# Reordering the opening of a modulated convolution kernel on all its engines

## The reference, cut to what matters

```python
s = style @ mw.T + mb
weight = SCALE * w * s[:, None, :, None]
demod = rsqrt(sum(weight * weight, axis=(2, 3)) + EPS)
weight = weight * demod[:, :, None, None]
# four layers: same, upsample + blur, same, blur + downsample; then x = x + out
```

## Time and profile before

| what | value |
|---|---|
| median of 3 runs (lowest, highest) | 1335.65 us (1335.02, 1335.79) |
| the profiled execution | 1336.1 us |
| its span in the trace | 1334.3 us |
| TensorE (PE) busy | 1301.2 us, 98% |
| VectorE (DVE) busy | 1150.0 us, 86% |
| ScalarE (ACT) busy | 842.1 us, 63% |
| GpSimd (POOL) busy | 347.3 us, 26% |
| DMA over the span | 152 GB/s |

### The profile page before, as it was taken

One profiled execution on the slowest core, in us unless ns is written; L12 is line 12 of the kernel. 1 busy time (PEld: TensorE's weight loads), 2 busy tenths in 40 slices (PEclk: granted clock), 3 DMA queues, 4 the chain that ended last, 5 costly groups with the idle time before them and its releaser, 6 DMA issues.

```text
span 1334.3 us, 20141 instructions
## 1 busy us (share of the span) xinstructions
PE 1301.2 (98%) x6565; PEld 1077.7 (81%) x6565; DVE 1150.0 (86%) x1855; ACT 842.1 (63%) x1528; POOL 347.3 (26%) x632
## 2 busy tenths in 40 slices
PE   7799999999999999999999999999999999999998
PEld 5588878888888788888888778888888878888887
DVE  6798879998988899989889789989888788898885
ACT  5656466656564666666655566566566667877774
POOL 3214221133122221124131221121522233323221
PEclk7899999999999999999999999999999999999999
DMA  9235655546554465454556445565554257655643
GB/s 312 77 100 163 166 146 125 159 149 186 170 149 113 135 186 170 141 172 121 162 172 171 140 112 158 164 178 162 164 146 124 93 121 190 186 170 146 177 121 99
DMA packets 95368, 203.38 MB, mean 152 GB/s; under 512 B 10720, under 2 KB 12256, under 8 KB 95264
## 3 DMA queue, kind: packets, MB, share of 16 engines
q1 hardware_dynamic: 94896, 201.81, 52.7%
q10 hardware_dynamic: 368, 0.28, 0.1%
HBM read 72.39 MB, written 67.24 MB: 105 GB/s over the span
## 4 chain that ended last, share of the span: by engine, by line
PE 75%; DVE 15%; ACT 4%; issue 3%; POOL 2%; DMA 1%; SPq 0%; ACTq 0%; DVEq 0%; POOLq 0%
PE ps L463 74%; ACT kp L750 2%; DVE gl L1067 2%; DVE gf L1031 2%; DVE zl L980 2%; DVE xl L974 2%; DVE X L989 1%; DVE vf L1010 1%; DVE gf L1037 1%; ACT xh L709 1%; DVE vl L1017 1%; DVE vh L1019 1%; POOL w3q L1279 1%; DVE v L1015 0%; DVE gf L1043 0%
## 5 line engine op out<-in xcount | busy, mean ns | idle before, releaser
L463 PE MATMUL ps<-zh,gh 128*128 128x512 f32 (+1 forms) x1028 | 411.1, 400 | 16.2 <-DVE zl L980 12.2
L463 PE MATMUL ps<-zl,gh 128*128 128x512 f32 (+1 forms) x1028 | 407.5, 396 | 0.0
L721 ACT ACTIVATE zh<-ps,t_bx 128x512 fp32r<-128x512 f32 x256 | 175.7, 686 | 271.4 <-PE ps L463 267.9
L463 PE MATMUL ps<-zh,gl 128*128 128x512 f32 (+1 forms) x1028 | 283.0, 396 | 0.0
L750 ACT ACTIVATE kp<-ps,t_T1s 64x256 f32<-64x256 f32 x512 | 213.5, 465 | 102.8 <-PE ps L463 99.5
L463 PEld LDWEIGHTS ps<-zh,gh 128*128 128x128 f32 x1028 | 195.0, 190 | 70.0 <-DVE zl L980 20.7
L989 DVE SCALAR_TENSOR_TENSOR X<-ps,t_D,X 128x512 f32<-128x512 f32 x255 | 190.0, 745 | 61.9 <-PE ps L463 35.4
L974 DVE SCALAR_TENSOR_TENSOR xl<-X,t_S,xh 128x513 fp32r<-128x513 f32 x256 | 202.1, 809 | 35.0 <-ACT xh L709 32.8
L980 DVE SCALAR_TENSOR_TENSOR zl<-ps,t_bx,zh 128x512 fp32r<-128x512 f32 x256 | 190.7, 745 | 48.1 <-ACT zh L721 45.2
L463 PEld LDWEIGHTS ps<-zl,gh 128*128 128x128 f32 x1028 | 195.4, 190 | 44.6
L463 PEld LDWEIGHTS ps<-zh,gl 128*128 128x128 f32 x1028 | 194.7, 189 | 45.4
(11 more groups left out here) (204 smaller groups left out, 1541.3 us busy)
## 6 DMA issues: line engine op xcount, KB each, us to landing
out_x<-X SPq DMA_DIRECT2D x255, 256.5 KB, 4.9
X<-out_x SPq DMA_DIRECT2D x96, 513.0 KB, 7.0
gh<-gh SPq DMA_DIRECT2D x127, 240.0 KB, 3.0
gl<-gl SPq DMA_DIRECT2D x127, 240.0 KB, 3.6
X<-x_in SPq DMA_DIRECT2D x32, 513.0 KB, 7.6
pk<-taps_in SPq DMA_DIRECT2D x3, 512.0 KB, 12.0
pk<-pack_in SPq DMA_DIRECT2D x3, 352.0 KB, 11.2
pk<-sets_in SPq DMA_DIRECT2D x4, 256.0 KB, 8.4
```

The costliest lines, as they stand in the source:

```text
L463: return pe.matmul(out_ap, a, b, start=first, stop=last, skip_group_check=True)
L721: act.activation(zh[n % 2][:, ZPAD:ZPAD + M], ps[:, ZP + n % 2, :], IDENT, bias=tab["bx"][:, k, b:b + 1]).then_inc(s["zhi"], 1)
```

## The change

The opening is written anew on every engine; the loops from iteration 2 on stay as they are, but for the place of `k_products(1)` and of the loads.

- TensorE makes `k_products(0)` in front of `conv0(0)` and `conv0(1)`, and `k_products(1)` behind `convg(0)` in place of behind `convg(1)`. `v_products(0)` may begin when the first half of `w3h` is there. Three groups of products whose result is not used (6, 6 and 20 of 256 columns on `w2h`) stand behind `v_products(0)`, `conv0(1)` and `v_products(1)`.
- ScalarE splits the second layer's weights first of all; `kev(0)` is in the usual order of two halves; the copies that give `gl` to the lower half (`glo_cross`) and of the outer taps (`taps_first`) move to it from VectorE.
- VectorE filters quad 0 in one go over both slots, and no longer in two; it takes `w0l` from GpSimd; `xnew(0)` comes before `xlo(3)`, and `vfull(1)`, `vlo(1)` before `zlo(1)`.
- GpSimd makes quad 1's `w3q` in front of `w1l`.
- SyncE issues `spread(0)` in iteration 1, in front of the store of sample 0, the loads of samples 16 to 23 behind it, and the weights of blocks 1, 2 and 3 (with the samples' ends) in iterations 4, 8 and 12.

```diff
@@ before build
+BLOCK_LOADS = {4: 1, 8: 2, 12: 3}
@@ SyncE
-            for n in range(2 * GS, NR * GS, 2):
-                load(n)
-            for k in range(1, NBLK):
-                sp.dma_start(pk[:, k, 0:PACK], pack[k]).then_inc(s_pack[k], 16)
-                sp.dma_start(pk[:, k, PACK:WALL], taps[k]).then_inc(s_taps[k], 16)
...
             for n in range(NN + 4):
-                if n == 2:
+                if n == 1:
                     spread(0)
+                    for m in range(2 * GS, NR * GS, 2):
+                        load(m)
+                if n in BLOCK_LOADS:
+                    k = BLOCK_LOADS[n]
+                    sp.dma_start(pk[:, k, 0:PACK], pack[k]).then_inc(s_pack[k], 16)
+                    sp.dma_start(pk[:, k, PACK:WALL], taps[k]).then_inc(s_taps[k], 16)
...
@@ TensorE, v_products(0): high parts start on the first half of w3h
+                if q == 0:
+                    pe.wait_ge(s["w2hi"], 1)
+                    pe.wait_ge(s["w3h0"], 1)
...
@@ TensorE, the order of the opening
             v_products(0)
-            conv0(0)
+            idle_products(6, filled)
             pe.wait_ge(s["z0"], 1)
             k_products(0)
+            conv0(0)
             conv0(1)
+            idle_products(6, filled)
             v_products(1)
+            idle_products(20, filled)
             for n in range(NN):
...
                 if n == 0:
                     convg(n)
+                    k_products(1)
...
-                if n in G_LATE:
-                    k_products(g_at(n))
@@ ScalarE, from the first weights on
+            act.wait_ge(s["w1t"], 16)
+            act.activation(w1d[:, 0, 0:K], w1T[:, 0], ACT.Copy).then_inc(s["w1d0"], 1)
+            act.activation(w1h[0:C, 0, 0:K], w1T[0:C, 0], ACT.Copy)
+            act.activation(w1h[C:128, 0, 1:K + 1], w1T[C:128, 0], ACT.Copy).then_inc(s["w1hi"], 1)
...
             w0hi(0)
-            w1hi(0)
-            xhi(0)
-            act.wait_ge(s["z0"], 1)
-            root(PARTS[1], 2)
-            vhi(0)
-            xhi(1)
-            w3hi(1)
-            zhi(0)
...
-            for j in (0, 2, 1, 3):
-                evict(0, j, 0)
-                ins = evict(0, j, 1)
...
-            ghi_first(0)
-            xhi(2)
-            zhi(1)
-            ghi_first(1)
-            ghi_rest()
-            vhi(1)
-            xhi(3)
-            root(PARTS[2], 3)
-            zhi(2)
-            xhi(4)
-            kev(1, 0)
-            kev(1, 1)
+            first_var(PARTS[2])
+            root(PARTS[1], 2)
+            w3hi(1)
+            vhi(0)
+            xhi(0)
+            xhi(1)
+            kev(0, 0)
+            root(PARTS[2], 3)
+            kev(0, 1)
+            zhi(0)
+            taps_first()
+            zhi(1)
+            xhi(2)
+            xhi(3)
+            ghi_first(0)
+            vhi(1, 0)
+            glo_cross(0)
+            vhi(1, 1)
+            ghi_first(1)
+            ghi_rest()
+            glo_cross(1)
+            kev(1, 0)
+            zhi(2)
+            kev(1, 1)
+            xhi(4)
             w3hi(2)
...
@@ VectorE, behind E1
             recip(PARTS[1], 2)
             vfull(0)
-            xlo(0)
-            vlo(0)
-            newton(PARTS[1], 2)
...
-            dve.wait_ge(s["kev0"], 1)
-            fir_first(slice(0, 1), "fir0")
-            xlo(2)
-            glo_first(0)
-            dve.wait_ge(s["kev"], 1)
-            fir_first(slice(1, 2), "fir")
...
+            newton(PARTS[1], 2)
+            vlo_first()
+            dve.scalar_tensor_tensor(T0["T1s"], dall[:, 0, :], 1.0 / BLUR_SUM, dall[:, 1, :], ALU.mult, ALU.mult) \
+                .then_inc(s["t1s"], 1)
+            dve.wait_ge(s["var0"], 2)
+            recip(PARTS[2], 3)
+            dve.wait_ge(s["w0hi"], 1)
+            dve.tensor_tensor(w0l[:, 0], w0f[:, 0], w0h[:, 0].bitcast(F32), ALU.subtract).then_inc(s["w0l"], 1)
+            xlo(0)
...
             xlo(1)
+            newton(PARTS[2], 3)
+            dve.wait_ge(s["kev"], 1)
+            fir_even(whole, both, first=True)
+            fir_odd(whole, both).then_inc(s["fir"], 1)
+            zlo(0)
+            vfull(1)
+            glo_first(0)
+            xlo(2)
+            vlo(1)
+            zlo(1)
+            glo_first(1)
+            xnew(0)
+            glo_rest()
             xlo(3)
-            xnew(0)
             zlo(2)
             xlo(4)
             for n in range(2, NN):
@@ GpSimd
-            sig(pool.tensor_tensor(w0l[:, 0], w0f[:, 0], w0h[:, 0].bitcast(F32), ALU.subtract), "w0l")
...
+            pool.wait_ge(s["e1"], 1)
             w3s(1)
+            w1low()
+            pool.wait_ge(s["t1s"], 1)
             w3lo(1)
@@ new functions of ScalarE
+            def taps_first():
+                act.wait_ge(s["fir0"], 1)
+                act.activation(gf[:, 0:NT:NT - 1], kp[:, 1:8:6], ACT.Copy).then_inc(s["gfe0"], 1)
+            def glo_cross(i):
+                act.wait_ge(s[("gl0a", "gl1a")[i]], 1)
+                act.activation(gl[C:128, 0, i, 1:NT + 1, :], gl[0:C, 0, i, 0:NT, :].bitcast(F32), ACT.Copy) \
+                    .then_inc(s[("gl0", "gl1")[i]], 1)
```

More of the change, by code:

```diff
@@ L521, in v_products @@
                 left, right = slice(0, 2), slice(2, 4)
-                pe.wait_ge(s["w2l"], k + 1)
-                if q >= 1:
-                    pe.wait_ge(s["kev"], q)
[L525 to L530, removed]
+                if q == 0:
+                    pe.wait_ge(s["w2hi"], 1)
+                    pe.wait_ge(s["w3h0"], 1)
+                    add(a[:, 0], wh[:, left, :], w3h[:, 0], first=True)
+                    add(a[:, 1], wh[:, right, :], w3h[:, 0])
+                    pe.wait_ge(s["w2l"], 1)
+                    add(a[:, 0], wl[:, left, :], w3h[:, 0])
+                    add(a[:, 1], wl[:, right, :], w3h[:, 0])
+                    pe.wait_ge(s["w3l0"], 1)
+                else:
+                    pe.wait_ge(s["w2l"], k + 1)
+                    pe.wait_ge(s["kev"], q)
+                    pe.wait_ge(s["w3h"], q + 1)
+                    add(a[:, 0], wh[:, left, :], w3h[:, 0], first=True)
+                    add(a[:, 0], wl[:, left, :], w3h[:, 0])
+                    add(a[:, 1], wh[:, right, :], w3h[:, 0])
+                    add(a[:, 1], wl[:, right, :], w3h[:, 0])
+                    pe.wait_ge(s["w3l"], q + 1)
                 add(a[:, 0], wh[:, left, :], w3l[:, :, :])
@@ L544, in k_products @@
                 pairs = ((k01, early, 0), (k23, late, 0), (k23, early, 1), (k45, late, 1))
-                pe.wait_ge(s["w1l"], k + 1)
+                if q == 0:
+                    pe.wait_ge(s["w1hi"], 1)
+                    pe.wait_ge(s["w1l0"], 1)
+                else:
+                    pe.wait_ge(s["w1l"], k + 1)
                 pe.wait_ge(s["vh"], q + 1)
@@ L553, in k_products @@
                 pe.wait_ge(s["vl"], q + 1)
+                if q == 0:
+                    pe.wait_ge(s["w1l"], 1)
                 add(k45, d[:, early, :], vh[:, 2, :, :])
@@ L735, in w3hi, with first_var, vhi @@
                 act.activation(w3h[:, :, :, :], w3q[:, :, :, :], ACT.Copy).then_inc(s["w3h"], 1)
[L737 to L742, removed]
+            def first_var(layers):
+                act.activation(var[:, layers, :], ps[:, EP + 1, layers.start * NB:layers.stop * NB]
+                               .rearrange("p (l b) -> p l b", b=NB), IDENT, bias=eps[:, 0:1], scale=SCALE * SCALE) \
+                    .then_inc(s["var0"], 1)
+            def vhi(q, part=None):
+                if part != 1:
+                    act.wait_ge(s["vf"], q + 1)
+                    if q >= 1:
+                        act.wait_ge(s["K"], q)
+                    act.activation(vh[:, 0:2, :, :], vf[:, 0:2, :, :], ACT.Copy).then_inc(s["vh"], 1)
+                if part != 0:
+                    act.activation(vh[0:C, 2, :, :], vf[0:C, 2, :, :], ACT.Copy).then_inc(s["vh2"], 1)
             def evict(q, j, part):
@@ L1031, in more, with fir_even @@
                 return dve.scalar_tensor_tensor(dve_out, kp[rows, of, i, :], factor, dve_out, ALU.mult, ALU.add)
-            def fir_even(rows, i):
-                step(dve.tensor_tensor(kp[rows, 1, i, :], kp[rows, 1, i, :], kp[rows, CORR, i, :], ALU.add))
-                settle()
+            def fir_even(rows, i, first=False):
+                corr = dve.tensor_tensor(kp[rows, 1, i, :], kp[rows, 1, i, :], kp[rows, CORR, i, :], ALU.add)
+                if first:
+                    corr.then_inc(s["fir0"], 1)
+                    dve.wait_ge(s["fir0"], 1)
+                else:
+                    step(corr)
+                    settle()
                 step(dve.scalar_tensor_tensor(gf[rows, 1:5, i, :], kp[rows, 1:8:2, i, :], BLUR_O, kp[rows, 3:10:2, i, :],
@@ L1051, in fir_odd @@
                 return more(rows, i, slice(3, 6), ODD, BLUR_E)
-            def fir_first(i, name):
-                rows = slice(0, 128)
-                fir_even(rows, i)
```

(2 more changed lines are left out.)

97 lines of the change are left out of this document (50 added, 47 removed), and 4 rows, old and new, of the table s.

## The result

The changed kernel took 1327.68 us (median of 4 runs, 1326.83 to 1328.47) against 1335.70 for the kernel before in the same session: a ratio of 0.9941, 95% interval 0.9924 to 0.9958. That is 8.0 us less; the forecast was 8.3 less, 1327.4. The profiled execution took 1327.4 us, 8.7 less than that of before.

A forecast was written before the change was run, and what follows sets the result against it. TensorE, busy 1121.11 of 1134 us from 200 us on, bounds the kernel, so an earlier start of its steady stream counts. -10.7 + 2.4 for the clock = -8.3 from 1335.65 gives 1327.4 us; range 1322.3 to 1331.0.

The forecast's parts named there:

- K(0) ends: TensorE's k_products(0) done at 15.7 us, before at 21.30: 5.6 us earlier.
- split of quad 2 ends: VectorE's last split of quad 2 ends at 50.5 us, 15.8 us after xlo(4) starts.
- `conv0(5)` starts: TensorE's first product from which both kernels run the same lists: 51.0 us against 61.66, 10.7 us earlier.
- clock at half: TensorE's clock falls between 47 and 50.4 us, in the pauses around k_products(2), and stays down 6.8 us.
- lost to the clock: Half of the 3.0 to 6.2 us at half clock behind conv0(5): 1.5 to 3.1, taken as 2.4 us.
- The wait for `zhi(4)`: VectorE's wait of 2.68 us before zlo(4) would go.
- The Newton steps beside GpSimd: VectorE's three Newton steps before it splits quad 0: 0.7 us each beside GpSimd's work, ending at 13.6 us.
- ScalarE's list of quad 1: ScalarE's work from vfull(1) at 25.2 us to the start of xlo(4) at 34.7: 9.5 us, the longest list.
- B: Rival: TensorE's clock stays up behind quad 2, so nothing is given back: 1324.9 us; 27%.
- C: Rival: half clock in the opening too, for convg(0) to convg(1), 2.5 us more: 1329.9 us; 13%.
- D: Rival: GpSimd holds VectorE up less (Newton steps, quad 1's filter), 3.3 us more gained: 1321.6 or 1324.0 us; 6%.
- E: Rival: spread copies land late, sharing DMA with the moved loads: once 1334.5 us, 3%; from the second on 1341.6, 4%.

The follow-up runs named there:

- the 20 products alone: Changed kernel with 20 unused products added only in front of k_products(2), none inside it: 1330.02 us, ratio 0.9940.
- the controls: The changed kernel itself, rerun without edits in two later sessions: 1330.85 and 1328.79 us.
- the second control: The changed kernel itself, rerun without edits in the last session: 1328.79 us, ratio 0.9947 against the kernel before.

## Why the prediction was right

Its steps against the profile, in us of the span:

| step | forecast | measured |
|---|---|---|
| V(0) ends | 10.6 | 10.67 |
| K(0) ends | 15.7 | 15.18 |
| evictions of quad 0 end | 19.3 | 18.86 |
| filter of quad 0 ends | 23.6 | 23.04 |
| `convg(0)` starts | 24.9 | 24.39 |
| second `glo_cross` ends | 30.0 | 29.83 |
| `xlo(4)` starts | 34.7 | 34.72 |
| split of quad 2 ends | 50.5 | 50.25 |
| `conv0(5)` starts | 51.0 | 51.23 |
| clock at half | falls in 47 to 50.4, 6.8 long | 48.58 to 55.42 |
| lost to the clock | 2.4 | 1.9 |

**What held.** The place where the two kernels become the same list was the right one, and the list that sets it: after the opening VectorE's, from `xlo(4)` to the split of quad 2. The run with `spread(0)` alone shows it from the side of before, the ones with K(0) and K(1) put back show the chain in front. The wait for `zhi(4)` went, as forecast. The loss to the clock was the forecast's most open term; it came, and in the two profiles with both of the pauses filled it was gone.

**What was off.** The Newton steps beside GpSimd were put at 0.7 each; they took 0.28, 0.58 and 0.29. `w1l`'s second half took 0.59 on GpSimd and not 1.12, so that less of GpSimd's work lay beside them. That is why everything from K(0) to `convg(0)` stood 0.5 earlier than forecast. ScalarE's list of quad 1 took 10.1 us and not 9.5 and ate it: it waited 0.93 us for the `gl` that the second `glo_cross` copies. At the other end `conv0(5)` stood 1.0 behind the split and not 0.5, as K(2)'s last products ran at half clock, which the sum counted from `conv0(5)` on only. VectorE's list from `xlo(4)` to the split took 15.5 and not 15.8. These misses have both signs and nearly cancel; that `conv0(5)` came within 0.2 us of its forecast is partly luck.

The kernel before had a third stay at 1.2 GHz, which the prediction doesn't count among its two:

```profile
14.00:15.00 1.00, 0.00 (x0) 0.00 (x0) 0.94 (x3) 0.19 (x1) 0.92 (x2) 0.75 1.00 369
...
21.00:22.00 1.00, 1.00 (x6) 0.87 (x6) 0.00 (x0) 0.64 (x2) 0.00 (x0) 0.83 1.03 382
```

From 14.50 to 21.34 us, by the means, it covered all of K(0), whose products took 3.4 us there and 2.5 in the changed kernel. So the two `conv0` and the late `w1l` and `w0l` are not all that K(0) was freed of: 0.9 of its 6.1 us is that shorter time, most of it the half clock.

**The sum.** 10.4 - 1.9 = 8.5 us at `conv0(6)`, against 8.7 between the two profiled executions. The loss is 1.9 and not half of the 4.2 us behind `conv0(5)`, for at 1.2 GHz `convg(4)`'s products stand 0.43 us apart (53.80 and 54.22) and at 2.4 GHz 0.23 (55.47 and 55.70): the prediction's "half of it is lost" was a little too much. The 0.2 that is left arises behind `conv0(6)`, where the two profiles differ near 1080 us as well; it is not assigned.

**The rivals.** B, in which the clock stays up, did not come by itself in any of the three profiles of the changed kernel; the rule of the Trainium skill, "TensorE: Matmul & The Clock Gate", section "HAM oscillation", which lays the fall to one long idle gap, does not agree with the run with the 20 products alone, where the clock fell at 50.6 in a pause of 2.2 us. C did not come in these three either; it came in variants: without the unused products, with the filter in two goes, and, at 17.4, with K(0) put back. D was partly there (Newton), and not in the filter of quad 1 (a step of 1.13 beside GpSimd). E did not come: `gl` of quad 1 was issued at 47.55, the block's loads at 48.68, and TensorE never waited for a copy.

**Which part made it.** Taken out alone, K(0) in front is worth 6.6 of the 7.3 us, K(1) in front 3.5, the filter in one go 1.8. The unused products (1.0), the later loads (0.6) and `spread(0)` alone on the old kernel (1.1) are not told from none by their times. The first three already add to more than the whole. The steps stand behind one another in one chain, and in these three profiles the step that was undone also moved the half clock; how much of each number is the clock is not separated. The work moved between engines (`w0l`, `glo_cross`, `taps_first`, GpSimd's order) was not taken out alone.

## What to carry to other kernels

To price a rewritten opening, look for the first instruction from which both versions run the same lists, and for the one engine whose list leads up to it without a wait; only what moves that list counts. In this kernel a pause of the tensor engine just in front of a stage that it bounds cost more than it seemed to: the pauses around K(2) were hidden behind VectorE, but the half clock that came with them cost up to 2.3 us, most of it in the stage behind. Products without use took that away when they stood in each piece of the pause, and gained nothing that the rows show when they stood in one of two. Before a small difference is ascribed to an edit, the same code has to be run again beside it: here its own start moved by 1.4 to 2.6 us. And where two medians differ by just what was expected, a point behind the change in both profiles tells whether it is for that reason.

## What the runs showed of the hardware

- The clock stayed at 1.2 GHz for 3.4 us (no unused products; the 20 alone; near 1080 us in eight profiles), 6.8 (both kernels, the controls) or 10.2 us (46.74 to 56.98 with the loads in front; 50.56 to 60.80 with K(1) put back). Each fall lay in a pause of TensorE or at most 1.4 us behind one; these pauses were 1.4 us (11.30, `spread(0)` alone) to 4.1 us long (26.92, no unused products).
- The same pause need not bring a fall each time: that of 2.2 us near 1080 us brought one in eight profiles of fourteen.
- The same code ran its first products at full speed from about 5 us on in one execution, and only from about 9 us on in another (ten products in 1.47 or 2.50 us), while the clock's column said 1.00; in the second control products at 12.77 us still stood 0.21 us apart. Of the profiled executions of the changed order, with its variants, two of twelve had the early start, of the old order both had; why is open.
- A step of VectorE's filter over 128 columns took 1.13 us beside an instruction of GpSimd (37.40, with GpSimd busy from 37.01 for 1.37) and 0.28 alone (59.12).
